# Diffusion step: the product of probabilities and rows in three parts, with the other tile's turning and mixing between them

## The reference

```python
def _top_p_attention(X, W1, W2, W3):
    q = X @ W1.T @ W2.T
    k = X @ W3.T
    probs = softmax(q @ k.T)                    # 2708 x 2708
    # keep each row's largest probabilities until their sum reaches 0.9
    A = probs * mask
    return A / max(A.sum(-1, keepdims=True), 1e-12)

R = (S + eye(N)) / row sums
for n in range(2):
    A = _top_p_attention(Xa, W1, W2, W3)
    Xf = R @ Xf
    Xa = A @ Xa
    Z = Z + Xf @ U1[n].T + Xa @ U2[n].T
```

## Time and profile before

| | us |
|---|---|
| median of 3 runs | 3207.61 |
| lowest and highest run | 3206.48, 3208.89 |
| profiled execution, its own time | 3207.16 |
| its span | 3205.4 |
| busy in the span: PE | 2308.1 (72%) |
| DVE | 2067.4 (64%) |
| ACT | 1261.7 (39%) |
| POOL | 533.7 (17%) |

### The profile page before, as it was taken

One profiled execution on the slowest core, in us unless ns is written; L12 is line 12 of the kernel. 1 busy time (PEld: TensorE's weight loads), 2 busy tenths in 40 slices (PEclk: granted clock), 3 DMA queues, 4 the chain that ended last, 5 costly groups with the idle time before them and its releaser, 6 DMA issues. The chain is left out here.

```text
span 3205.4 us, 46057 instructions
## 1 busy us (share of the span) xinstructions
PE 2308.1 (72%) x14618; PEld 1674.3 (52%) x14618; DVE 2067.4 (64%) x4921; ACT 1261.7 (39%) x2067; POOL 533.7 (17%) x1503
## 2 busy tenths in 40 slices
PE   2388888488628999968615753758628099999999
PEld 2366666376406877856304642546427044444458
DVE  5578888623347777781366778677783767777741
ACT  4355555321456666621454653657511300000000
POOL 0000000000034443410053332335310000000000
PEclk9699999799759999989757887889769599999999
DMA  1222221053100000001000000000000300000012
GB/s 43 111 91 91 86 82 66 1 191 121 39 16 16 21 26 18 25 13 53 16 1 10 10 10 10 10 10 14 10 5 10 144 2 0 0 0 0 0 40 95
DMA packets 49254, 120.85 MB, mean 38 GB/s; under 512 B 5904, under 2 KB 24624, under 8 KB 45744
## 3 DMA queue, kind: packets, MB, share of 16 engines
q1 hardware_dynamic: 49072, 118.83, 10.9%
HBM read 93.85 MB, written 24.97 MB: 37 GB/s over the span
## 5 line engine op out<-in xcount | busy, mean ns | idle before, releaser
L1311 PE MATMUL bank<-kH,qHL 128*128 128x512 f16 (+1 forms) x264 | 109.9, 416 | 421.6 <-ACT step_E L1387 403.0
L1806 DVE SCALAR_TENSOR_TENSOR fil_acc<-bank,fil_node,fil_acc 128x256 f32<-128x256 f32 x682 | 330.0, 484 | 108.5 <-PE bank L1874 95.7
L1311 PEld LDWEIGHTS bank<-kH,qHL 128*128 128x128 f16 (+1 forms) x264 | 27.2, 103 | 480.6 <-ACT step_E L1387 449.8
L1872 PE MATMUL bank<-parts_in,fil_xTh 128*128 128x512 f16 x704 | 267.8, 380 | 0.0
L1873 PE MATMUL bank<-parts_in,fil_xTh 128*128 128x512 f16 x704 | 267.4, 380 | 0.0
L1874 PE MATMUL bank<-parts_in,fil_xTl 128*128 128x512 f16 x704 | 267.3, 380 | 0.0
L1387 ACT ACTIVATE step_E<-bank 128x512 f32<-128x512 f32 (+1 forms) x264 | 131.5, 541 | 321.3 <-DVE step_recips L1734 229.7
L1503 DVE MAX8 step_top<-step_E 128x8 f32<-128x2708 f32 x44 | 131.2, 2982 | 171.4 <-ACT step_E L1387 168.2
L1408 ACT ACTIVATE step_junk<-step_E,step_first 128x2708 fp8e4<-128x2708 f32 x88 | 224.6, 2552 | 15.0 <-ACT step_first L1414 9.5
L1378 ACT ACTIVATE step_PT<-bank 128x512 f32<-128x512 f32 (+1 forms) x264 | 125.8, 578 | 252.1 <-PE bank L1301 252.1
L1333 PE MATMUL bank<-H,step_PT 128*128 128x256 f32 x968 | 216.2, 379 | 0.0
(11 more groups left out here) (347 smaller groups left out, 5327.6 us busy)
## 6 DMA issues: line engine op xcount, KB each, us to landing
gat_A<-in_adj SPq DMA_DIRECT2D x22, 1408.0 KB, 6.0
step_a<-adjT SPq DMA_DIRECT2D x44, 352.0 KB, 2.9
gcn_raw<-in_L_W SPq DMA_DIRECT2D x16, 512.0 KB, 4.7
split<-gcn_halves SPq DMA_DIRECT2D x16, 512.0 KB, 3.4
parts_in<-split SPq DMA_DIRECT2D x4, 2048.0 KB, 19.3
adjT<-gat_a SPq DMA_DIRECT2D x22, 352.0 KB, 2.2
gcn_a<-adjT SPq DMA_DIRECT2D x22, 352.0 KB, 3.9
out_a<-adjT SPq DMA_DIRECT2D x22, 352.0 KB, 2.9
```

The lines of the kernel that those rows point to most:

```text
L1311: last = pe.matmul(l_bank[n % 2][:, 0:m], cols(qHL, t, 128), k[:, c:c + m], start=part == 0, stop=part == 1)
L1806: c(dve.scalar_tensor_tensor(out=acc[k][:], in0=ps, scalar=node[k][:, n:n + 1], in1=acc[k][:], op0=ALU.mult, op1=ALU.add))
L1872: pe.matmul(w_bank[n % 4][:], xTh[k][:, x], wh[:, blk], start=c == 0, stop=False)
```

## The change

`attend` gets three parts in place of two. The parts end at the bounds of chunks, so that they hold 8, 8 and 6 of the 22 blocks, where both held 11. The first waits for two evicted chunks of PT (three before), the second for four and the third for all six. The turning of the other tile moves behind the first part, from its place right behind the transposes. Its mixing moves behind the second part, so behind 16 blocks and not 11. The last block still raises `pv_ready`.

```diff
             def attend(p, j, n):
                 t = p * 2 + j
-                pe.wait_ge(pT_done, t * NCH + (NCH // 2 if n == 0 else NCH))
-                for i in range(T * n // 2, T * (n + 1) // 2):
+                pe.wait_ge(pT_done, t * NCH + NCH * (n + 1) // 3)
+                for i in range(CHUNKS[NCH * n // 3][0], sum(CHUNKS[NCH * (n + 1) // 3 - 1])):
                     last = pe.matmul(pvf_bank[j][:, 0:D], PT[:, i * 128:i * 128 + 128], srcA[:, i * D:i * D + D],
                                      start=i == 0, stop=i == T - 1)
-                if n == 1:
+                if n == 2:
                     last.then_inc(pv_ready, 1)
...
                 return [*chunks[0:2], rows[0], *chunks[2:4], rows[1], *chunks[4:], rows[2],
-                        (2, lambda p, q: all_transposes(p, j)), (mixed, lambda p, q: turn(p, 1 - j)),
-                        (2, lambda p, q: attend(p, j, 0)), (mixed, lambda p, q: mix(p, 1 - j)),
-                        (2, lambda p, q: attend(p, j, 1))]
+                        (2, lambda p, q: all_transposes(p, j)), (2, lambda p, q: attend(p, j, 0)),
+                        (mixed, lambda p, q: turn(p, 1 - j)), (2, lambda p, q: attend(p, j, 1)),
+                        (mixed, lambda p, q: mix(p, 1 - j)), (2, lambda p, q: attend(p, j, 2))]
```

## The result

The change makes the kernel slower: 3317.69 us median (3313.68 to 3320.03, 4 runs) against 3207.38 us (4 runs), a ratio of 1.0342 with a 95% interval of 1.0324 to 1.036. That is 110 us more; the forecast was 123 us more, in a range of 3280 to 3362 us. The profiled execution has a span of 3314.7 us where it was 3205.4.

The account below looks back on a forecast made before the run. Bound: PE's third chunk to transposes, then ACT's list; in step 1 ACT sets first halves, DVE second. Step 0 37.7, step 1 48.9, clock 20.8 and 16.0: 123.4 us on 3207.2, so 3331 us, range 3280 to 3362.

Parts of the forecast that it names:

- The loop: A half's length is set by PE from the third chunk to the transposes, then ACT's list from PT to logits.
- The stall of step_vT: ACT stands still for the late turning, 2.81 us in a half of step 0 and 3.42 in step 1.
- The mix in step 1: DVE's path begins at the mix, 2.16 us later: eight second halves, the first half-pair and the drain.
- The clock in step 1: Slower PE stretch after 5.1 us waits inside eight pairs of step 1: 8 x 2.0 = 16.0 us.
- The clock in step 0: Slower PE stretch from third chunk to T after waits near 3 us: 1.60 in 13 halves, 20.8 us.
- Step 0 without the clock: Seven second halves 18.9 us, seven first halves 14.5, DVE's pair 2.16 and the last half 2.16: 37.7 us.
- the pair that DVE sets: Step 0's pair with the 4.7 us wait for MAX8, set by DVE's path from the mix: 2.16 us longer.
- The rival of the clock that stays up in step 0: Clock falls only in step 1: 3310 us; 24 in 100 together with the clock staying up everywhere, 3294.
- The long fall: PE's clock falls for longer in each half, so the clock term doubles: 3368 us; 14 in 100.
- The hidden stall: ACT's stall is hidden, only DVE's waits for the mix count: 26 us, 3233 us; 7 in 100.
- the gain: PE starts its product 0.43 us sooner in 44 halves, 19 us faster: 3188 us; 3 in 100.
- the third rival: ACT's stall does not show; DVE's mix waits of 2.16 us cost 26 us, giving 3233; 7 in 100.

Follow-up runs that it names:

- The filled kernel: Changed kernel with products of identity and weights before the third chunk of logits, five in step 0 and nine in step 1; 3303.58 us, ratio 1.0294.
- the neighbours' move: Kernel before the change, with the third part of the neighbours' product moved behind the transposes and the turning; 3200.91 us, ratio 0.9981.
- the small loads: Kernel with the mixing late and turning in place, with loads of the graph's rows cut from 352 KB to 16 KB; 3247.33 us, ratio 1.0129.

## Why the prediction was right, and where it was off

1. **The loop.** PE from the third chunk to the transposes, then ACT's list, was named as what sets a half. The late turning alone costs 75 us though on PE only places changed, and ACT's copies behind the exponential take the turning's cost away again, so this is shown. In step 1 the division into a first half set by ACT and a second set by DVE is shown by the two single moves: 5.0 and -0.1 us with the turning late, 0.00 and 2.0 with the mixing late.
2. **The stall of step_vT.** 2.81 and 3.42 us were forecast. The gaps read 2.57 and 3.2, from records that overlapped by 0.15 before, so the added time is some 2.7 and 3.4. The filled kernel shows 3.31 us in the length of a half of step 1.
3. **The mix in step 1.** 2.16 us in ten places were forecast, 21.6 us; the mixing alone costs 20.3. This term and the stall's eight times 3.42 make the forecast's 48.9 us for step 1 without the clock; the 64.6 measured, less eight times 1.84 of the clock, are 49.9.
4. **The clock in step 1.** 2.0 us each were taken from the restarts; 1.84 were measured.
5. **The clock in step 0, the term that was off.** "I therefore charge 1.60 to each of 13 halves" held in price (1.67 here) but not in number: 7 more fell than before, not 13, and the granted clock of the stretch came to 0.96 and not 0.93. After waits of 2.8 to 3.7 us the clock fell in some halves and not in others with waits of the same length; the forecast had made it certain from two rows. This is 20.8 - 11.7 = 9 us of the 13 by which the sum was too high.
6. **Step 0 without the clock.** 37.7 us were forecast and 47.0 - 11.7 = 35.3 are left. The sum is right in part by luck, since its terms missed in opposite ways. Without the clock the seven second halves are 21.8 us longer (forecast 18.9), the seven first ones 11.5 (forecast 14.5) and the pair that DVE sets 0.2 (forecast 2.2). Why the first halves took less than their term is not shown. In the second halves the path over the reciprocals was level with ACT's list, while the forecast let only ACT's list set them. In the changed kernel that path ends up to 0.7 us later than ACT's list (five waits, 3.0 us), because DVE's stretch had grown. With both paths late by about the same, the cost is that of the later one. That is why the two single moves cost 37.0 and 28.6 us in step 0 and both together 47.0, while in step 1 39.3 and 20.3 add up to the 64.6 within 5 us. The clock is not the reason: without it the three numbers of step 0 are 28.7, 17.3 and 35.3.

The rival of the clock that stays up in step 0 came nearer to the total (3310) than the forecast, though the clock did fall there in 9 of 16 stretches. After waits near 2 us nearly none fell, after waits near 3 us about half in the changed kernel, and after waits of 5 us all eight. The Trainium skill (TensorE: Matmul & The Clock Gate, "HAM oscillation — how this bites in real kernels") says that only a gap of some length drops the clock. That agrees with the runs in kind, but not where it sets the bound: with the turning late all 16 waits of step 0 are too short by it, 3.13 us at most, and 7 of them were followed by a fall. The long fall did not come in the changed kernel: its falls cost 1.67 us in step 0 and 1.84 in the mean of step 1. The hidden stall and the gain are refuted by the late turning. One price was too low on a path that was seen: the third rival took the late mix as 26 us, and alone it costs 48.

## What to carry to other kernels

Where an engine's list is written by hand, a small step moved behind a long one is priced at what stands behind its receiver, not at what the moving engine does: PE's work is the same here, and ACT and DVE each stood still for its new order. Look for the second path that ends level with the first; there a delay of either shows, and an advance of one alone shows hardly at all, as the neighbours' move did in step 0. A step whose result an engine waits for belongs as early as its inputs are there; here that made the same three parts a gain of 0.6%.

## What the runs showed of the hardware

- After a wait of PE of 2.8 to 3.7 us the granted clock fell in 9 of 16 halves in the changed kernel, and in 7 of 16 with the turning late, where nearly all waits read 2.85 to 2.94. It did not fall after any of the eight waits of 1.93 us that step 1 has with ACT's copies behind the exponential, and it fell after 3 of 8 waits of 2.3 to 2.8 us in step 0 with the small loads. Equal waits can go either way. The share is not the same in all kernels: in step 0's second halves it fell after 7 of 8 waits of 3.0 to 3.7 us with the mixing late, and after 8 of 8 of 2.75 to 3.80 with ACT's copies behind the exponential. One fall cost 1.67 us in the changed kernel's step 0, and up to 2.85 with the mixing late (7.61 us from the third chunk to the transposes where 4.76 is the full clock's). With products put into the wait, so that 0.6 to 1.6 us were left, none of 16 fell.
- DVE's stretch between the reduced flag and the next instruction behind the branches takes 3.6 us in the mean of the kernel before, where a load of 352 KB is issued 1.6 to 2.0 us into it. It takes 4.5 in the mean and up to 4.9 in the changed kernel, where that load is issued 0.2 to 0.6 us before it begins, and 3.8 in the mean where the load is 16 KB. It holds a packet of 8 KB on an instruction queue each time, and ends 1.85 to 2.11 us behind that packet's start. A branch on a path that sets the end is not a fixed price.
